# Last expert layer of a decoder: from all experts on all tokens to tokens sent to their two experts

## The reference, cut to what matters

```
xf = x.reshape(-1, 128)                              # 2048 tokens
shared_out = (silu(xf @ sw1) * (xf @ sw3)) @ sw2     # one shared expert, hidden 256
logits = xf @ router_w.T + experts_bias              # 8 experts
rw, sel = top_k(logits, 2);  rw = softmax(rw)        # the two best and their weights
cw = (one_hot(sel, 8) * rw[..., None]).sum(axis=1)
g = einsum('td,edh->teh', xf, w1);  u = einsum('td,edh->teh', xf, w3)
moe_out = einsum('te,teh,ehd->td', cw, silu(g) * u, w2)
return moe_out + shared_out
```

## Time and profile before

| | us |
|---|---|
| median of 3 runs | 2753.91 |
| the profiled execution, its own time | 2760.46 |
| span of its profile (first to last instruction) | 2758.7 |
| last stage, from 2544.4 to 2758.7 in that span | 214.3 |
| TensorE busy in the whole span | 2275.7 |
| granted TensorE clock, mean of the span | 0.916 |

### The profile page before, as it was taken

The page is one execution under the profiler, slowest core; times in us unless marked ns, Lnnn a source line. Parts: engine busy times, 40 slices in busy tenths (PEclk is TensorE's granted clock), DMA queues, the critical chain, the costliest instruction groups (busy, mean ns, idle before and its releaser), DMA issues. The chain is left out here.

```text
span 2758.7 us, 36333 instructions
## 1 busy us (share of the span) xinstructions
PE 2275.7 (82%) x13683; PEld 1298.5 (47%) x13683; DVE 1480.9 (54%) x3428; ACT 1144.7 (41%) x2178; POOL 218.5 (8%) x387
## 2 busy tenths in 40 slices
PE   5779678887899999999877799995477777687997
PEld 4445423333454555455545466664233334344565
DVE  3447577775533102230334566776866776565545
ACT  2335356664333222322232455553255556355221
POOL 1110210000211001110200100001200000100001
PEclk8889789999999999999977899997689999799999
DMA  2000000000400000000000000001000000000000
GB/s 67 1 1 1 1 0 1 1 1 1 176 1 1 0 1 0 1 1 0 1 1 1 1 1 1 1 1 60 0 1 1 1 1 1 1 1 1 1 1 16
DMA packets 10677, 24.16 MB, mean 9 GB/s; under 512 B 1992, under 2 KB 4988, under 8 KB 9993
## 3 DMA queue, kind: packets, MB, share of 16 engines
q1 hardware_dynamic: 9457, 20.81, 2.2%
q10 hardware_dynamic: 1048, 1.02, 0.1%
HBM read 20.76 MB, written 1.05 MB: 8 GB/s over the span
## 5 line engine op out<-in xcount | busy, mean ns | idle before, releaser
L1447 ACT ACTIVATE H<-PS,cols_l1f_sb 128x512 f32<-128x512 f32 x160 | 109.9, 687 | 333.6 <-PE PS L1353 209.6
L1359 PE MATMUL PS<-H,cols_l1f_sb 128*128 128x512 f32 x384 | 172.3, 596 | 13.9 <-ACT H L1447 13.9
L687 DVE TENSOR_REDUCE l1aM<-PS 128x2 f32<-128x1024 f32 x128 | 151.6, 1218 | 36.5 <-PE PS L443 35.6
L1560 DVE SCALAR_TENSOR_TENSOR R<-PS,probs,R 128x128 f32<-128x128 f32 x112 | 31.5, 344 | 248.3 <-PE PS L1401 248.1
L152 POOL TENSOR_SCALAR rstd<-MV 128x2 f32<-128x2 f32 (+1 forms) x100 | 28.9, 289 | 1601.2 <-DVE MV L124 1587.5
L605 ACT ACTIVATE l1aE<-PS 128x512 f32<-128x512 f32 x256 | 143.8, 595 | 22.4 <-PE PS L472 19.6
L1543 DVE BATCH_NORM_STATS2 s<-PS 128x6 f32<-128x512 f32 x64 | 44.7, 698 | 199.7 <-PE PS L1379 199.7
L605 ACT ACTIVATE l3aE<-PS 128x512 f32<-128x512 f32 (+3 forms) x256 | 102.2, 434 | 78.6 <-PE PS L476 75.7
L1400 PEld LDWEIGHTS PS<-cols_l1f_sb,H 128*128 128x128 f32 x1024 | 126.1, 191 | 17.3 <-issue 15.0
L1400 PE MATMUL PS<-cols_l1f_sb,H 128*128 128x128 f32 x1024 | 130.7, 280 | 0.8 <-DVE R L1560 0.8
L1353 PE MATMUL PS<-XT,cols_l1f_sb 128*128 128x512 f32 x256 | 124.8, 617 | 3.9 <-ACT XT L1434 3.9
(11 more groups left out here) (579 smaller groups left out, 5053.3 us busy)
## 6 DMA issues: line engine op xcount, KB each, us to landing
cols_l1f_sb<-in_cols_l1f SPq DMA_DIRECT2D x16, 256.0 KB, 11.3
cols_l1f_sb<-in_cols_l1f SPq DMA_DIRECT2D x4, 1024.0 KB, 10.8
cols_l3f_sb<-in_cols_l3f SPq DMA_DIRECT2D x1, 3460.0 KB, 13.8
cols_l1f_sb<-in_cols_l1f SPq DMA_DIRECT2D x4, 512.0 KB, 9.7
cols_l2x_sb<-in_cols_l2x SPq DMA_DIRECT2D x1, 1154.0 KB, 14.6
out<-X SPq DMA_DIRECT2D x4, 256.0 KB, 2.3
cols_l2f_sb<-in_cols_l2f SPq DMA_DIRECT2D x1, 561.0 KB, 9.9
terms<-in_terms ACTq DMA_DIRECT2D x1, 516.5 KB
```

The lines of the kernel that those rows point to most:

```text
L687: v.tensor_reduce(M[:, m % 2, qt, 2 * hp:2 * hp + 2], PS[:, bank:bank + 2, 0:kc], AX, ALU.max, negate=True).then_inc(pair_free, 1)
L1359: ins = mm(o, m[:, c0:c0 + P], h1(e, b)[:, c, :], start=(c == 0), stop=(c == FC - 1))
L1447: nc.scalar.activation(o, PS[:, n % 2, :], ACT.Gelu, bias=bias).then_inc(acted, 1)
```

## The change

The stage computes the shared expert for all tokens as before, and each token's two chosen experts alone. It does so in these steps:

1. SyncE writes `X` to a DRAM tensor `rows`. TensorE makes all 64 tiny routing records first; VectorE ranks the experts of all 16 token tiles.
2. A list is built from the choices, between pieces of the shared expert's work: matrix products with a triangular matrix count how many tokens went to each expert before a given one (`count_tensor`); VectorE turns counts into tiles of 128 slots, the expert of each tile (`experts_vector`) and each token's slot (`places_vector`); one-hot matrices and 64 products (`spread_vector`, `list_tensor`, `list_vector`) turn that round into `of` (which row fills a slot) and `to` (where a slot's result goes). There are always 39 tiles: 4096 choices fill 32, and 7 more are room for rounding up per expert. An unused slot reads some row and writes to a place that nobody reads.
3. For each tile i GpSimd gathers its 128 rows by an indirect DMA into `XG`; TensorE transposes them (`turn`), ScalarE copies (`take`), TensorE multiplies with w1 and w3 (`up`, four products of width 128), ScalarE and VectorE make the hidden values (`gate`, `hidden`), TensorE multiplies with w2 (`down`, two products), VectorE copies the result (`result`), and GpSimd scatters its rows to a DRAM tensor `placed` by another indirect DMA. SyncE reads the tile's expert from SBUF into a register (`value_load`) and loads that expert's 384 KB from DRAM into one of 4 buffers `WB`. `XG` and `O` have 4 buffers too.
4. When all is scattered SyncE loads `placed` back (8 DMAs of 256 KB), VectorE adds both results of each token to `R`, weighted, and normalises.

The pack `l3f` shrinks to the shared expert (388 KB), and a new pack `disp` of constants is loaded beside it. The core of the diff (declarations, constants and unchanged pieces are cut; `norm_stats` also gets a form without its first addition):

```
+class Dispatch:
...
+    TILES = B * S * 2 // P + 7
...
+    def count_tensor(self, bank, counted):
...
+        mm(bank[:, 0:(N + 1) * 8], self.earlier_b[:, :], self.marks[:, :, :].rearrange("p n e -> p (n e)"), start=True, stop=False)
+        for n in range(N):
+            ins = mm(o[:, n + 1:N + 1, :], self.k.ones_b, self.marks[:, n:n + 1, :].broadcast_to([P, N - n, 8]),
+                     start=False, stop=(n == N - 1))
...
+    def spread_vector(self, step, tiled, spread):
...
+        v.tensor_tensor(self.at_tile[:, :, :], self.iota_b[:, 0:T].unsqueeze(1).broadcast_to([P, 2 * N, T]),
+                        self.tile_b[:, :].unsqueeze(2).broadcast_to([P, 2 * N, T]), ALU.is_equal).then_inc(tiled, 1)
+        step(v.tensor_tensor(self.at_row[:, :, :], self.iota_b[:, :].unsqueeze(1).broadcast_to([P, 2 * N, P]),
+                             self.row_b[:, :].unsqueeze(2).broadcast_to([P, 2 * N, P]), ALU.is_equal))
...
+        v.tensor_tensor(self.high[:, :, :], self.at_tile[:, :, :],
+                        self.ids_b[:, :].unsqueeze(2).broadcast_to([P, 2 * N, T]), ALU.mult).then_inc(spread, 1)
...
+    def list_tensor(self, bank, listed):
...
+        for m in range(last + 1):
+            mm(o, self.at_row[:, m, :], self.high[:, m, :], start=(m == 0), stop=False)
+            ins = mm(o, self.at_row[:, m, :], self.low[:, m, :], start=False, stop=(m == last))
...
+    def gather(self, out, i):
+        g = self.k.nc.gpsimd
+        return g.indirect_dma_start(out, None, self.rows, bass.IndirectOffsetOnAxis(ap=self.of[:, i:i + 1], axis=0))
+
+    def scatter(self, src, i):
+        g = self.k.nc.gpsimd
+        return g.indirect_dma_start(self.placed, bass.IndirectOffsetOnAxis(ap=self.to[:, i:i + 1], axis=0), src, None)
...
+def experts_two(k, w, d, weights, rows, placed, out):
...
+    RING, AHEAD = 4, 4
...
         @block.sync
         def _(sp):
+            sp.dma_start(rows.rearrange("(n p) d -> p n d", p=P), k.X[:, :, :]).then_inc(rows_out, 16)
+            sp.wait_ge(found, 1)
+            for i in range(T):
+                e = sp.value_load(disp.expert_i[0:1, i:i + 1], min_val=0, max_val=7 * P)
+                if i >= RING:
+                    sp.wait_ge(o_ready, i - RING + 1)
+                sp.dma_start(WB[:, i % RING, :], weights[bass.ds(e, P), :]).then_inc(loaded[i % RING], 16)
+            for j in range(RING):
+                sp.wait_ge(scattered[j], 16 * len(range(j, T, RING)))
+            for b in range(BT):
+                for c in range(2):
+                    lo = c * B * S + b * S
+                    sp.dma_start(YB[:, c, b * NT:(b + 1) * NT, :],
+                                 placed[lo:lo + S, :].rearrange("(t p) d -> p t d", p=P)).then_inc(back[b], 16)
...
+            shared_up(0)
+            pe.wait_ge(lg_copied, 1)
+            pe.wait_ge(marked, 1)
+            disp.count_tensor(COUNTS, counted)
+            shared_down(0)
+            shared_up(1)
+            shared_down(1)
+            shared_up(2)
+            pe.wait_ge(spread, 1)
+            pe.wait_ge(lowered, 1)
+            disp.list_tensor(LIST, listed)
+            shared_down(2)
+            shared_up(3)
+            shared_down(3)
...
+            turn(0)
+            turn(1)
+            up(0)
+            for i in range(T):
+                if i + 2 < T:
+                    turn(i + 2)
+                if i + 1 < T:
+                    up(i + 1)
+                down(i)
...
         @block.gpsimd
         def _(pool):
+            pool.wait_ge(known, 1)
+            pool.wait_ge(rows_out, 16)
+            for i in range(AHEAD):
+                disp.gather(XG[:, i % RING, :], i).then_inc(gathered[i % RING], 16)
+            for i in range(T):
+                pool.wait_ge(o_taken, i + 1)
+                disp.scatter(O[:, i % RING, :], i).then_inc(scattered[i % RING], 16)
+                if i + AHEAD < T:
+                    pool.wait_ge(x_turned, i + AHEAD - RING + 1)
+                    disp.gather(XG[:, (i + AHEAD) % RING, :], i + AHEAD).then_inc(gathered[(i + AHEAD) % RING], 16)
             for b in range(BT):
                 k.norm_gpsimd(pool, b, b)
...
+            for b in range(BT):
+                dve.wait_ge(back[b], 32)
+                for c in range(2):
+                    for t in range(NT):
+                        n = b * NT + t
+                        step(v.scalar_tensor_tensor(k.R[:, b, t, :], YB[:, c, n, :], pw[:, 2 + c, n:n + 1], k.R[:, b, t, :], ALU.mult, ALU.add))
+                    step.wait()
+                k.norm_vector(dve, None, step, normed, b, b)
```

More of the change, by code:

```diff
@@ L117, in norm_stats @@
         for h in HALVES:
-            step(v.tensor_tensor(self.R[:, b, h], y[:, h], x[:, h], ALU.add))
-            step.wait()
+            if y is not None:
+                step(v.tensor_tensor(self.R[:, b, h], y[:, h], x[:, h], ALU.add))
+                step.wait()
             for t in range(h.start, h.stop):
@@ L2202, with body @@
 IC = [(0, P), (P, P), (2 * P, 96)]
-def experts_two(k, w, out):
+def experts_two(k, w, d, weights, rows, placed, out):
     nc, PS = k.nc, k.PS
[L2208 to L2223, removed]
+    N, T = BT * NT, Dispatch.TILES
+    RING, AHEAD = 4, 4
+    COUNTS, LIST = PS[:, 6, :], PS[:, 7, :]
+    def body(block, routed, lg_copied, pair_spread, exped, g_ready, silued, eo_done, d_ready, y_done, steps, normed, stored,
+             marked, counted, found, tiled, spread, lowered, listed, known, rows_out, x_turned, x_taken, gu_ready, gate_done,
+             h_done, o_ready, o_taken, *rings):
+        back, loaded, gathered, scattered = (rings[j * RING:(j + 1) * RING] for j in range(4))
@@ L2224, in body @@
         SG = k.sb("SG", [P, 2, S])
         EO = k.sb("EO", [P, 2, 2, S])
[L2226 to L2261, removed]
-                            ins = mm(PS[:, 4 + n % 2, t * P:(t + 1) * P], EO[:, n % 2, c, t * P:(t + 1) * P],
-                                     w["w2"][:, (e * 2 + c) * P:(e * 2 + c + 1) * P], start=(c == 0), stop=(c == 1))
-                    ins.then_inc(d_ready, 1)
@@ L2279, in _, with shared @@
         def _(act):
-            for u in order:
-                kind, e, b, c = u
-                if kind == "G":
-                    n = at[u]
+            def shared(b):
+                for c in range(2):
+                    n = 2 * b + c
                     act.wait_ge(g_ready, n + 1)
@@ new lines, in result @@
+            def result(i):
+                dve.wait_ge(o_ready, i + 1)
+                if i >= RING:
+                    dve.wait_ge(scattered[i % RING], 16 * (i // RING))
+                v.tensor_copy(O[:, i % RING, :], PS[:, 4 + i % 2, 0:P]).then_inc(o_taken, 1)
+            for i in range(T):
+                hidden(i)
+                if i:
+                    result(i - 1)
+            result(T - 1)
+            dve.wait_ge(exped, 1)
+            step(v.tensor_scalar(pw[:, 2, :], pw[:, 1, :], 1.0, None, ALU.add))
@@ L2362, in quantised_ffn @@
+    k.stage("l3f", ["routed", "lg_copied", "pair_spread", "exped", "g_ready", "silued", "eo_done", "d_ready", "y_done", "steps", "normed",
+                    "stored", "marked", "counted", "found", "tiled", "spread", "lowered", "listed", "known", "rows_out", "x_turned",
+                    "x_taken", "gu_ready", "gate_done", "h_done", "o_ready", "o_taken",
+                    *(f"{s}{j}" for s in ("back", "loaded", "gathered", "scattered") for j in range(RING))], body)
 def quantised_ffn(k, w, ahead):
```

331 lines of the change are left out of this document (263 added, 68 removed).

## The result

The changed kernel takes 2771.83 us, the median of 6 runs (2764.63 to 2778.16), against 2756.35 for the kernel before in 6 runs (2751.64 to 2761.53): a ratio of 1.0057, 95% interval 1.0036 to 1.0078. It is slower; the forecast was 2744, faster. The time lies in the range, on the side of the rivals.

What follows compares the result with a forecast made beforehand. It took TensorE to bound the old stage and a two-tile gather-scatter circle the new tiles: 48.6 + 121 + 34.4 = 204.0 us against 214.3, so about 2744 us, range 2713 to 2788.

Steps and rivals of the forecast that it cites:

- What bounded the kernel before, and what goes: Last stage: bound by TensorE; 32 of its 36 units go, 167 us of TensorE work.
- The circle: Tiles: result, scatter, gather, transpose, products, next result form a loop moving two tiles a turn, 6.37 us; 19 turns, 121 us.
- g: GpSimd's issue of one indirect DMA, gather or scatter: taken as 1.1 us.
- L: A gather's landing beyond its issue: taken as 2.0 us.
- 2g + L: Scatter issue, gather issue and landing in a turn: 4.2 us, with 2.7 as low end and 6.2 as high.
- C: Fixed part of a turn (transpose, products, copy, three hops between engines): 2.17 us at full clock, 3.62 at the lower.
- the first rival: Tiles run at 1.2 GHz: a turn of 8.1 us, time 2777; low clock or long round trip, chance 0.31.
- break-even of 6.9 us a turn: Turn of two tiles at which the change gains nothing: 2g + L of 4.7 us at full clock.
- The weights: 384 KB a tile land in 3.3 us, needed 6.4 us after their buffer is free: hidden, costed at nothing.
- SyncE: Register load, address and issue cost nothing; rival: over 3.2 us a tile, at 4.0 a time of 2775, chance 0.07.
- Ahead of the tiles: From the stage's start: list known at 37.5 us, first result taken at 48.6.
- Behind the tiles: Last scatter, loads back, four sequences on VectorE (24.9 us) and the end (3.2): 34.4 us in all.

Runs made afterwards that it cites:

- e2_order: Changed kernel with GpSimd issuing the gather of tile i+4 ahead of the scatter of tile i, nothing else: 2727.4 us, ratio 0.9888.
- e4_ring8: Changed kernel with eight `XG` buffers and eight gathers ahead instead of four, order of the lists kept: 2714.5 us, ratio 0.9845.
- e6_filler_dve: Changed kernel with three unread extra products a tile on TensorE and VectorE's result of tile i-1 ahead of hidden of tile i: 2756.8 us, ratio 0.9998.
- e8_no_weights: Changed kernel with weights loaded for the first four tiles alone, later tiles reusing them: 2753.1 us, ratio 0.9987.
- e10_best: e4_ring8 with ten buffers and gathers ahead, VectorE's result before hidden, an early GpSimd drain, and statistics ahead of the previous scaling: 2722.5 us, ratio 0.9885.
- e9_all_late: Changed kernel with the transpose of i+2 behind down(i), gate(i+1) ahead of take(i+2), result(i-1) ahead of hidden(i): 2739.0 us, ratio 0.9932.

## Why the prediction was wrong, point by point

**What bounded the kernel before, and what goes.** Right: the TensorE work went, and TensorE isn't what paces the tiles.

**The circle.** Right in its two tiles a turn, in the wait that it shows, and in its path but for one stretch on VectorE (below): the earlier trace rows had no such wait, the changed kernel has TensorE waiting 27 times for `XG`. e2_order (44 us by order alone) and e4_ring8 (57 us by room alone) show that it bound.

**g and L.** g = 1.1 for an indirect DMA with its gap, and L = 2.0. Measured, GpSimd needs 2.26 from the scatter's start to the gather's end (0.98 + 0.30 + 0.97), where 2g was 2.2; a gather lands 2.0 behind the end of its issue in the mean. Both right, and the 2g + L that I took as likeliest was the one measured. The Trainium skill's price, about 2.15 in all ("DMA: Bandwidth & Descriptors", section on the SWDGE path), is too low for an indirect DMA here: from issue to landing the gathers take 2.4 at least and 2.6 in the median, and the scatters 2.9 in the median:

```profile
DMA to landing us min/median/max: 2.4/2.6/4.1
```

**C: the term that failed.** The forecast had 2.17 for everything else of a turn at the full clock. In the mean over the even tiles a turn is 0.30 (result to scatter) + 2.26 + 2.34 (end of the gather's issue to transpose) + 3.09 (transpose to result) = 7.99, against 6.37. The excess of 1.62 is:
- The clock, 0.79: the way from transpose to result took 3.09 where the same lists at the full clock take 2.30. This is the first rival, and it decided as that rival said: "from about 37% of the tiles' stretch at the lower level", where 60% was measured. I had given it 0.31 and taken the full clock as likeliest on the strength of the earlier trace rows, where stretches equally busy stand at both levels; such rows could not decide it. The Trainium skill's rule ("TensorE: Matmul & The Clock Gate", section on oscillation), which the prediction cited for this rival, named the right side, but the trace agrees with it only in part: its loop has products that are shorter than the wait and turns cold in every round, while here TensorE was busy for 94.0 of the 146.7 us, and the clock went down and up again within the stretch.
- VectorE's order, 0.30: what is left at the full clock, 2.30 against the 2.01 of e6_filler_dve, since the path is `up`, `gate`, `hidden`, result, and not `up`, `down`, result. The forecast's own terms give 1.99 for this way. I had read the order of TensorE's and GpSimd's lists, not VectorE's. The two causes overlap: taken away alone, at the clock that the changed kernel had, the order is worth 0.05.
- Hops between engines (from the end of one's work to the start of the next one's), 0.43: from the result to the scatter 0.30 and from the landing to the transpose 0.31, where I had 0.27 for three.
- g by 0.06, L by 0.03.

In all, 146.7 in place of 121: 19 turns by 7.72, since the last two take 10.85 together, where the 17 ahead of them take 7.99 each. The break-even of 6.9 us a turn stood in the prediction, 0.53 above its own turn, and the clock alone used that up. With what was measured around the tiles, 80.3 us, break-even is 7.05; e6_filler_dve, with the first two causes mostly gone, has 7.13 by the same count and came out even.

**The weights.** Costed at nothing for `WB`'s own waits: right, none. But "hidden" left out what they do to others: e8_no_weights shows 0.51 a turn in the gathers' landing and, with the clock, 0.4 more. The L = 2.0 came from loads that ran nearly alone and was right by luck, as a mean of short landings and long ones; the first gathers, ahead of this traffic, landed 1.5 to 1.6 behind their issue (three of the first four).

**SyncE.** Right: its register load, address and issue together took 1.38 us for the first tile of the changed kernel (2565.11 to 2566.48) and 1.10 for each of the next three, under the 3.2 of the rival. But the earlier trace rows show no full queue: the issue of 2.43 is SyncE's third of the program, and five later ones (at 8.21 to 10.02), with more DMAs just ahead of them, took 0.36 to 0.43.

**Ahead of the tiles.** Forecast 37.5 for the list and 48.6 for the first result, measured 31.6 and 43.2. The small operations came in near their rows (routing 7.3 for 6.8, at a clock of 0.51 as feared; the earlier trace rows do not show that cold start, but the trace of before has 0.50 from 2543 to 2549), but the 64 list products are spaced by 0.025, not 0.076:

```profile
L303 PE MATMUL PS<-l3f_high,l3f_at_row x32: 179/180/192, 2577.3 to 2578.9; 128*128 128x39 bf16 x32
```

39 columns, not 128: I had taken a price by record and not by width. And a dependent small step takes 0.26 with its wait, not 0.30 to 0.35: the 18 of experts and places lie between 2562.64 and 2567.28.

**Behind the tiles.** Forecast 34.4, measured 37.1. From result 38 to the first addition 6.9 (6.3), four sequences in 23.5 (24.9), and the end 6.6 behind the last row instead of 3.2. The timeline's last lines:

```profile
2768.17 0.60 DVE L136 TENSOR_SCALAR X<-R,MV,rstd 128x128 f32<-128x128 f32 x2 [0.41 <-POOL rstd L155]
2768.80 0.38 SPq L2406 DMA_DIRECT2D out<-X  x1
```

The store lands 2.3 later, at 2771.1; the span ends at 2775.4. GpSimd's sequencer is in its drain from 2767.28 to 2774.52. That term, 3.4 us, nobody could read from the kernel before, where the drain takes 0.81.

## What to carry to other kernels

With in-order engine lists, buffers do not set how many tiles are under way: write down, for each engine's list, what stands ahead of the result that restarts the loop, since the longest way round passes through whichever list has the newest tile's work first (here it moved from TensorE's to ScalarE's and VectorE's, and left for GpSimd's pace only with the gather ahead of the scatter, or with more gathers ahead). A loop of short products between waits for data ran mostly at the low clock here: price its fixed part at that level too, and take a margin thinner than the difference as even. Price every way through the lists at both levels, since which one is the longest changes with the clock. A load that nobody waits for still lengthens the small transfers beside it, and an order that shortens a waiting loop can slow one that is bound elsewhere (VectorE's, 7.4 us less in one and 16 us of tiles more in the other, for a reason that stays open).

## What the runs showed of the hardware

- An indirect DMA of 128 rows of 512 bytes holds GpSimd 0.97 (gather) or 0.99 us (scatter), with 0.30 between one and the next, so 1.28 us each: the floor of every version here.
- A gather lands some 1.5 us behind the end of its issue with little other traffic, and 2.5 in the mean with a load of 384 KB in flight all the while (12 gathers of the changed kernel).
- The first drain on GpSimd behind indirect DMAs takes 7.2 to 8.5 us and a second one 0.95; in the kernel before, without such DMAs, the same drain takes 0.81. Placed beside another wait it costs nothing, at the end of the program 3.4 us. Indirect DMAs are not the only cause of a long one: both kernels also have one around an all-reduce near 1912 and 1919 us, of 9.97 and 6.00.
- The step in clock is worth 1.06 us of the way from transpose to result with the lists of the changed kernel (3.36 to 2.30), and 1.36 with the result ahead of `hidden` (3.37 to 2.01): what ScalarE and VectorE add does not shorten with it.
- Taking away 0.51 us a turn of landing brought 18.7 us, not 9.7, and the granted clock was higher (0.86 for 0.70).
- In e10_best and e9_all_late a semaphore that TensorE sets rose up to 5.1 us behind the recorded end of its products, for ScalarE and VectorE alike, and only in these two. Nothing here says why.
